# Attention on TensorE: the output product of the pair two back moved from behind a pair's first key unit to in front of it

## The reference, cut to what matters

```python
x = x + _L0_xattn_ref(_layernorm(x), ctx, ctx, Wq, Wk, Wv, Wo, bo, mask)
x = x + _L0_ffn_ref(_layernorm(x), ln_g, ln_b, rW, rb, W1, b1, W2, b2)

# attention:
qh, kh, vh = split_heads(q @ Wq), split_heads(k @ Wk), split_heads(v @ Wv)
dots = jnp.einsum('bhid,bhjd->bhij', qh, kh) * SCALE        # masked, causal
attn = jax.nn.softmax(dots, axis=-1)
out = jnp.einsum('bhij,bhjd->bhid', attn, vh)
return out @ Wo + bo                                        # the "output product"
```

## Time and profile before

| | |
|---|---|
| median of 3 runs | 987.0 us (986.75 to 987.83) |
| the profiled execution | 988.03 us, its span in the trace 986.3 us |
| PE busy | 881.8 us, 89% of the span |
| DVE busy | 732.0 us (74%) |
| ACT busy | 629.3 us (64%) |
| POOL busy | 500.6 us (51%) |

### The profile page before, as it was taken

How to read it: one execution, slowest core, us unless ns; L and a number is a source line. 1 busy time by engine, 2 the same in 40 slices (tenths; PEclk the granted TensorE clock), 3 DMA queues, 4 the chain that set the end, 5 groups by cost and what they waited for, 6 DMA issues and landing times. The chain is left out here.

```text
span 986.3 us, 32438 instructions
## 1 busy us (share of the span) xinstructions
PE 881.8 (89%) x10928; PEld 744.1 (75%) x10928; DVE 732.0 (74%) x2217; ACT 629.3 (64%) x1352; POOL 500.6 (51%) x584
## 2 busy tenths in 40 slices
PE   6899899999999999999999999999855999999800
PEld 5688788888888887888888788888744888888700
DVE  3986778788887878888787888877755666666438
ACT  3678576686776767677676767768513556666525
POOL 3612445364644536464454646443453777777720
PEclk7999999999999999999999999999876999999955
DMA  9100101010010101101010110000013333333259
GB/s 282 38 24 2 37 11 38 5 37 22 26 32 11 37 5 37 32 17 35 8 37 5 40 32 14 24 8 18 10 33 102 111 105 106 102 107 104 74 198 331
DMA packets 55856, 56.69 MB, mean 57 GB/s; under 512 B 7383, under 2 KB 48769, under 8 KB 55809
## 3 DMA queue, kind: packets, MB, share of 16 engines
q1 hardware_dynamic: 46192, 37.01, 12.8%
q0 software_dynamic: 8704, 17.97, 5.0%
q10 hardware_dynamic: 913, 1.15, 0.3%
HBM read 32.76 MB, written 23.36 MB: 57 GB/s over the span
## 5 line engine op out<-in xcount | busy, mean ns | idle before, releaser
L735 ACT ACTIVATE pr<-pr 128x512 f32<-128x512 f32 x128 | 80.7, 631 | 192.3 <-DVE pr L1246 192.3
L856 PE MATMUL bank<-cTh,Ah 128*128 128x256 f32 x584 | 183.0, 313 | 14.9 <-DVE cTl L1232 7.9
L645 POOL DMA_INDIRECT mixed<-kf,ix_i x144 | 139.8, 971 | 56.5 <-issue 35.3
L678 ACT ACTIVATE kf<-bank 128x512 f32<-128x512 f32 x256 | 154.2, 604 | 6.2 <-PE bank L860 4.1
L860 PE MATMUL bank<-cTh,Al 128*128 128x256 f32 x512 | 146.1, 285 | 0.0
L857 PE MATMUL bank<-cTl,Ah 128*128 128x256 f32 x512 | 145.6, 284 | 0.0
L552 POOL DMA_INDIRECT slots<-zrow,slot_ix x120 | 121.5, 1013 | 34.2 <-issue 28.2
L489 POOL TENSOR_TENSOR idle_p<-half 128x1 f32<-128x1 f32 x114 | 40.4, 354 | 192.0 <-DVE slot_ix L1341 163.4
L1256 DVE TENSOR_TENSOR pr<-pr,ri 128x512 f32<-128x512 f32 x128 | 132.1, 1032 | 4.4
L856 PEld LDWEIGHTS bank<-cTh,Ah 128*128 128x128 f32 x584 | 112.7, 193 | 29.6 <-issue 17.9
L983 PE MATMUL bank<-wo_s,oT 128*128 128x128 f32 x1024 | 127.4, 278 | 2.4 <-ACT oT L731 2.4
(11 more groups left out here) (197 smaller groups left out, 1938.1 us busy)
## 6 DMA issues: line engine op xcount, KB each, us to landing
kf<-slots SPq DMA_DIRECT2D x72, 130.0 KB
xs<-in_x_dram SPq DMA_DIRECT2D x16, 256.0 KB
c_in<-in_ctx_dram SPq DMA_DIRECT2D x16, 256.0 KB, 3.0
kf<-mixed SPq DMA_DIRECT2D x8, 512.0 KB, 5.0
vf<-mixed SPq DMA_DIRECT2D x8, 512.0 KB, 5.2
out_dram<-xs SPq DMA_DIRECT2D x16, 256.0 KB, 4.3
mixed<-kf,ix_i POOLq DMA_INDIRECT x144
slots<-zrow,slot_ix POOLq DMA_INDIRECT x120, 2.4
```

The lines of the kernel that those rows point to most:

```text
L645: pool.indirect_dma_start(out=mixed, out_offset=bass.IndirectOffsetOnAxis(ap=ix_i[buf][:, j:j + 1], axis=0), in_=y_sb[buf][:, j, :], in_of ...
L678: act.activation(kfs[par][:, 2 * u:2 * u + 2, :], ring[gr.bank(name)].rearrange("p (h t) -> p h t", h=2), ACT.Copy).then_inc(act_ev, 1)
L856: pe.matmul(ps, lh, rh, start=True, stop=False)
```

## The change

The call of `project` and its condition move up by one unit: they stand behind the value unit V{i}0 and in front of the wait for `cTl` and the key unit K{i}0. It is the same for all places i, in the loop and outside it. At pairs 0 and 1 there is no output product, and at pairs 62 and 63 there is no key unit.

```diff
@@ -1047,12 +1047,12 @@
                     if first and i == 0:
                         pe.wait_ge(pro_l, 5)
                     value_unit(gr, f"V{i}0", i)
+                    if not (first and i < 2):
+                        project(n - 2, gr.done(f"O{i - 1}1", 0) if i else kept.done("O31", 0))
                     if keyed:
                         if i % 2 == 0:
                             pe.wait_ge(dve_ev, gr.done(f"P{i}", 1))
                         key_unit(gr, f"K{i}0")
-                    if not (first and i < 2):
-                        project(n - 2, gr.done(f"O{i - 1}1", 0) if i else kept.done("O31", 0))
                     if not (first and i == 0):
                         t_half(gr, f"T{i}0", n - 1, 1 - par, 0)
                     if keyed:
```

## The result

The changed kernel takes 972.4 us (median of 4 runs, 970.5 to 972.7) against 986.9 us: ratio 0.9851, 95% interval 0.9833 to 0.9869. Its profiled execution took 972.5 us with a span of 970.7.

The account below looks back on a forecast made before the run. PE sets the pace in the attention stage. Twelve groups 7.3 us plus group 2's 2.6 less 0.6 for pairs without a wait give 9.3 us off 987.0: 977.7 us, range 973.5 to 982.5.

Parts of the forecast that it names:

- the two waits for `cTl`: PE ahead of K0 at i = 0 and i = 2: both waits vanish, hidden by the output product.
- rival with a wait: B: half the gain goes to ACT's K30 copy, 980 to 985, 0.13; C: DVE sets the pace, no change, 0.06.
- step (2): PE's new borders: V0 to product costs nothing extra; product to key unit makes K0 0.79 us instead of 0.72.
- step (6): Margins: `oT` copies 1 us early; K0 1.85 us later for ACT; DVE gets the product 0.7 us sooner, keeping abreast.
- step (4): Pair 8: PE idle 2.67 to 1.06 us, pair 9's scores 2.2 us earlier (1.6 to 2.5); group 2 gains 2.6.
- (3): Steady groups: V0 and K0 together take 1.59 us; a group gains 0.61 us, twelve groups 7.3 us.
- (5): Pairs without a wait, 2 to 7, 60 and 61, lose 0.07 us each, 0.6 us in all.
- rival E's first half: Border from output product to key unit costs nothing, 3.2 us more gain; E as a whole, under 974, chance 0.06.
- a K0 of 0.72: Sign in the changed profile: K0 to T0 at 0.72 us instead of 0.79 would show a free border.
- E's second half: Earlier product pulls DVE and ACT forward, shrinking K32's 0.30 us wait, 14 x 0.2 us; E reaches 972, chance 0.06.
- bound under the sum: Over the 46 pairs paying openly, a free border means 3.2 us more gain, a dearer one 1.4 us less.
- The limit by ACT's list behind K00: Pair 8: ACT copies K00 at 118.52 behind the second exponential; its list ends the second seed by 122.2.

Follow-up runs that it names:

- even_only: Kernel before with the output product in front of the key unit at i = 0 and 2 only: 974.0 us, ratio 0.9852.
- behind_t0: Kernel before with the output product moved one unit later, behind K0 and T0: 992.3 us, ratio 1.0049.
- odd_only: Kernel before with the output product in front of the key unit at i = 1 and 3 only: 980.9 us, ratio 0.9916.
- i1_only: Kernel before with the output product in front of the key unit at i = 1 only: 978.8 us, ratio 0.9910.
- before_again: Kernel before, unchanged, run once more with its own trace: 987.0 us, ratio 0.9989.
- low_first: Kernel before, PE order kept; on DVE at i = 2 the context's low part goes ahead of the routing: 993.4 us, ratio 1.0054.
- k30_first: Changed kernel with ACT's copy of K30 at i = 3 ahead of the second exponential: 968.9 us, ratio 0.9810 to the kernel before.
- k30_third: Same program as k30_first, run again on another chip like the first: 966.6 us, ratio 0.9791 to the kernel before.
- after_third: Changed kernel run a third time, on a chip like the first: 972.6 us, ratio 0.9838 to the kernel before.
- the three of the slower chip: Changed kernel, k30_first's program, and changed kernel with low_first's diff: 1054.4, 1054.1 and 1064.6 us, where the kernel before took 1064.4.
- ahead_v0: Output product one step further than in the changed kernel, in front of V0, right behind the scores: 974.4 us, ratio 0.9866 to the kernel before.

## Why the prediction was wrong

The direction and the place were right: the two waits for `cTl` vanished, the output product runs at once, DVE and ACT kept up, and no rival with a wait came up. The size was wrong, and the largest part of it by a price in step (2) that does not exist: it was put at 0.07 us a pair, 3.2 us in all, and measured as nothing. A term was missing in step (6), and step (4) was left incomplete. With the price of step (2) at nothing the sum would have given 974.5 us, inside the stated range. What carried the measured time below the range is in good part the 2.2 us of the clock behind pair 63, which are luck.

**Step (2), the price of the new neighbours, and with it (3) and (5).** This is the step that failed. I read K1's 0.79 against K0's 0.72 as a price of following plain fp32 matmuls and charged 0.07 to every K0. The rows show where it comes from. The end of the product in the changed kernel, pair 37, from a timeline cut close around it, and then the same for the kernel before, where T0 follows:

```profile
422.11 0.28 PE L983 MATMUL bank<-wo_s,oT 128*128 128x128 f32 x1
422.14 0.36 PE L856 MATMUL bank<-cTh,Ah 128*128 128x256 f32 x1
422.34 0.28 PE L857 MATMUL bank<-cTl,Ah 128*128 128x256 f32 x1
```

```profile
429.33 0.50 PE L983 MATMUL bank<-wo_s,oT 128*128 128x128 f32 x3
429.66 0.27 PE L955 MATMUL bank<-ident,pr 128*128 128x128 f32 x1
```

Fifteen of the product's matmuls start 0.11 us apart. If a transpose follows, the sixteenth does too ((429.66 - 429.33) / 3 = 0.11). If a key unit follows, that unit's first row starts 0.03 us behind the sixteenth and its second 0.20 later. 0.03 + 0.20 is what 0.11 + 0.12 is: the record only draws the line between the two blocks 0.08 us earlier. T0 has the same: it takes 0.36 for four transposes 0.11 apart. So the border is free, as rival E's first half had it, although I looked for its sign in a K0 of 0.72. E's second half, a shorter wait of K32, did not come (0.29 us, it was 0.30). even_only and behind_t0 show the same by pairs whose time doesn't depend on the order. Without the charge a group gains 0.27 + 0.57 = 0.84 us, 10.1 us in twelve, and pairs 2 to 7 lose nothing: together about 3.2 us of the miss, the further gain that I had worked out as a bound under the sum and gave too little weight.

**Step (6), DVE's earlier product.** I took it for a thing that keeps the others abreast. It is a second cause. At i = 1 DVE waits 0.75 us for the product and then works through statistics, softmax and routing to `cTl` of i = 2, with no idle time but two of 0.16 us behind instructions of its own. (The list of DVE's work ahead of the prediction leaves out the statistics at i = 1, which come behind the addition, L1237, and the routing at i = 3.) The addition in pair 33, before and then changed, and the whole wait of DVE for the product in the changed kernel, which was 36.7 us in 48 times:

```profile
387.07 0.29 DVE L1237 TENSOR_TENSOR xs<-bank,xs 128x128 f32 x1 [0.74 <-PE bank L983]
```

```profile
380.47 0.29 DVE L1237 TENSOR_TENSOR xs<-bank,xs 128x128 f32 x1
```

```profile
DVE xs L1237 <- PE bank L983: 7.9, 2, 5.7
```

The addition starts 5.04 us behind the pair's scores before and 4.33 in the changed kernel, and `cTl` ends 2.57 and 1.87 us behind the next pair's scores: the 0.7 us arrive in full. odd_only and i1_only remove the wait at i = 2 by this path alone, even_only by the cover alone; either suffices, so the two don't add up. behind_t0 runs the path backwards and pays. Where it does add is pair 62, in the last group, whose router unit (L920) waits for POOL's `zrow`: 1.06 us before, 0.24 in the changed kernel, 0.22 in i1_only and 0.96 in even_only. That is 0.7 us, and the term was missing from the sum. That the path to POOL runs through the statistics of i = 1 is argued from the lists; the runs show only that the place i = 1 decides it.

**Step (4), pair 8.** From V00 to pair 9's scores it took 10.91 us, not 10.4, a gain of 1.65 us instead of 2.2. DVE's standstill, 2.69 us in the earlier trace rows, was 3.08 us in this trace, and `cTl` came 3.92 us behind V00's start instead of 3.50:

```profile
112.73 0.50 PE L856 MATMUL bank<-Vh,cTh 128*128 128x512 f32 x1
...
116.78 0.38 PE L856 MATMUL bank<-cTh,Ah 128*128 128x256 f32 x1 [1.30 <-DVE cTl L1232]
...
123.64 1.50 PE L1000 MATMUL bank<-kf,zT 128*32 128x256 f32 x24
```

```profile
114.08 0.87 DVE L1167 BATCH_NORM_STATS2 st<-xs 128x6 f32 x4 [3.08 <-issue]
```

The limit by ACT's list behind K00 was right in kind. The miss of 0.55 us is of the size by which executions differ: pair 8 took 13.99 and 14.45 us in the traces of before, 12.34 and 12.04 in those of the changed kernel, so the gain lies between 1.65 and 2.4 us, with the forecast's 2.2 inside.

The reading of the earlier trace rows overlooked something, though. The granted clock falls to its half in pair 8 of the kernel before, behind the long wait of PE, and stays whole in the changed one. The output product and the transposes behind it, before, and then the windows of the whole pair, before and changed:

```profile
116.88 2.76 PE L983 MATMUL bank<-wo_s,oT 128*128 128x128 f32 x16
119.47 0.60 PE L955 MATMUL bank<-ident,pr 128*128 128x128 f32 x4
```

```profile
110.37:124.36 13.99, 11.32 (x143) 9.62 (x142) 9.48 (x24) 7.53 (x17) 8.97 (x11) 0.88 0.20 60
```

```profile
111.30:123.64 12.34, 10.49 (x144) 8.42 (x143) 9.27 (x24) 6.60 (x16) 9.18 (x11) 1.00 0.22 66
```

K00 takes 1.44 us there (116.88 - 115.44) and the product 2.59 (119.47 - 116.88) instead of 0.72 and 1.78, and ACT waits 1.01 us for T00. So a part of the gain in pair 8 is clock and not only idle time; no run separates the two. Of the six traces with the product behind K00 at i = 0, the clock fell there in five (before, before_again, odd_only, i1_only, low_first; idle 2.67 to 3.17 us ahead of K00) and stayed whole in behind_t0 (2.71); in none of the nine with the product in front of K00 did it fall (idle at most 1.68 us). In odd_only, i1_only and low_first it stayed at its half for longer (0.78 in the mean of the pair instead of 0.88) and pair 8 took 15.55, 15.44 and 15.80 us; this makes their pair 8 dearer than that of before, since the three edits touch no pair at i = 0.

**Not in the prediction at all: TensorE's clock behind pair 63,** 2.2 us. It fell there in both traces of before and in neither of the two of the changed kernel on such a chip. But it also stayed whole in low_first, which is slower than before and has its PE order. It fell in odd_only and i1_only, in the changed kernel on the slower chip, and in one of two traces of the same program, k30_first and k30_third. PE's idle times in this stretch are alike to a few hundredths up to the fall: 1.52 to 1.53 us ahead of the third product of a value unit, 7.3 us behind pair 63's scores, in all fifteen traces. So nothing ties these 2.2 us to the product's place; what decides them in an execution stays open.

Together: 13.2 us in pairs 2 to 62 and 2.3 us from pair 63's scores to the last pair's transposes, less 1.0 us by which the start took longer in this trace; a further 1.0 us lies between there and the end. In before_again that last part is 0.6 us shorter than in the changed kernel, so this is the spread of executions. What the change itself is shown to earn are the 13.2 us of pairs 2 to 62 (13.9 between before_again and after_third, by pair 8).

## What to carry to other kernels

A price read from one block of a pipelined timeline is a price only if the block ahead of it has not become cheaper by as much: sum start to start over both sides of a border before charging it. An instruction placed early has two ways to pay, by covering a wait on its own engine and by waking the engine that waits for its result; follow the second through that engine's list to the next thing somebody waits for. When a wait stands at a copy late in an in-order queue, as K32's did, look for what stands idle ahead of it in that queue: one step there brought about 5 us more in the pairs. And before a difference of two traces is explained, compare the granted clock stretch by stretch: here it made 2.2 us that belong to no edit, and a part of pair 8's time that looked like work.

## What the runs showed of the hardware

A plain fp32 matmul of 128x128 followed by a key unit's first matmul is recorded with a start-to-start of 0.03 us instead of 0.11, and the matmul behind the border with 0.20 instead of 0.12; the sum is the same.

Behind pair 63, with the same work, TensorE was granted the half clock for some time in ten traces: those that reach pair 63's scores at 692.7, 696.5, 701.0 and 701.4 us (14.2 to 14.5 us for the stretch), behind_t0 at 705.8 (13.7), ahead_v0 at 689.6 and k30_first at 684.2 (13.5), and the three of the slower chip (13.9 to 14.2). It was granted the whole clock in those that reach them at 683.7, 688.7, 689.6, 690.5 and 709.9 (12.0 us). The time of arrival alone doesn't order them, and one program stands on both sides.

Ahead of K00 in pair 8 PE stood idle for 2.67 to 3.17 us in five traces in which the granted clock then fell to its half, for 2.71 us in one in which it did not, and for at most 1.68 us in the nine in which it stayed whole.
